# Experts' limits by bisection: marks on GpSimd, counts in TensorE, one step a group, and the weights' scaling on ScalarE

## What is computed

```
xn  = layernorm(x)
out = x + attention(xn) + experts(xn)
# attention: 16 heads of 16, k, q, v = xn @ W_kqv + b; causal, with slopes[h] * (j - i)
# added to the scores; softmax; y @ W_proj + b_proj
# experts: probs = softmax(xn @ Wg) over 8 experts, T = 4096 tokens, cap = T // 8 = 512
_, top_idx = top_k(probs.T, cap)          # each expert marks its 512 likeliest tokens
tok2exp = likeliest expert among those that marked the token, else the likeliest of all
out += probs[t, tok2exp] * gelu(xn @ W1[e]) @ W2[e]      # F = 512, for e = tok2exp[t]
```

## Time and profile before

| what | us |
| --- | --- |
| median of 3 runs | 610.05 |
| lowest, highest | 603.38, 613.67 |
| the profiled execution | 612.12 |
| its span in the trace | 610.4 |

### The profile page before, as it was taken

The page is one execution under the profiler, slowest core; times in us unless marked ns, Lnnn a source line. Parts: engine busy times, 40 slices in busy tenths (PEclk is TensorE's granted clock), DMA queues, the critical chain, the costliest instruction groups (busy, mean ns, idle before and its releaser), DMA issues.

```text
span 610.4 us, 13176 instructions
## 1 busy us (share of the span) xinstructions
PE 500.1 (82%) x4807; PEld 287.9 (47%) x4807; DVE 406.3 (67%) x829; ACT 324.6 (53%) x608; POOL 400.1 (66%) x556
## 2 busy tenths in 40 slices
PE   1989996578878889889888987887897798787876
PEld 1555652223334435344344444443356587665764
DVE  5887669998998897988998967530113545344543
ACT  4455651055656665766756646555643445353542
POOL 4877627567666796876867878884413476555555
PEclk9999997568989999999999899898699999888999
DMA  8999988322424432524325236538445344443510
GB/s 262 270 240 280 318 280 277 107 62 62 124 63 120 137 122 88 159 79 134 97 81 150 80 118 204 185 93 304 126 88 130 89 102 107 96 94 94 101 53 34
DMA packets 94902, 85.58 MB, mean 140 GB/s; under 512 B 36883, under 2 KB 84883, under 8 KB 94831
## 3 DMA queue, kind: packets, MB, share of 16 engines
q1 hardware_dynamic: 82088, 59.64, 34.2%
q0 software_dynamic: 7360, 18.80, 10.5%
q10 hardware_dynamic: 5392, 6.31, 3.4%
HBM read 42.26 MB, written 37.95 MB: 131 GB/s over the span
## 4 chain that ended last, share of the span: by engine, by line
PE 45%; DVE 34%; issue 10%; ACT 5%; POOL 3%; another core or an unknown queue 2%; DMA 1%; DVEq 0%; ACTq 0%; POOLq 0%
DVE mx L987 14%; PE ps L1378 8%; PE ps L1246 8%; PE ps L1358 5%; PE ps L1408 5%; PE ps L1540 4%; DVE mx L982 4%; PE ps L1530 3%; PE ps L1531 3%; PE ps L1283 2%; DVE pr_all L1204 2%; DVE pr_all L1209 2%; ACT pr_all L857 2%; PE ps L1353 2%
## 5 line engine op out<-in xcount | busy, mean ns | idle before, releaser
L857 ACT ACTIVATE pr_all<-ps 128x512 f32<-128x512 f32 x320 | 179.2, 597 | 124.9 <-PE ps L1358 110.1
L987 DVE TENSOR_REDUCE mx<-ps 128x2 f32<-128x768 f32 (+1 forms) x192 | 156.3, 862 | 15.6 <-PE ps L1283 7.9
L1358 PE MATMUL ps<-qs,ks 64*128 64x384 f16 (+3 forms) x512 | 110.6, 318 | 10.2 <-ACT pr_all L857 9.3
L711 POOL TENSOR_SCALAR_AFFINE_SELECT pr_all<-pr_all 128x256 f32<-128x256 f32 (+1 forms) x168 | 70.1, 445 | 67.0 <-ACT pr_all L857 66.4
L1378 PE MATMUL ps<-pr_all,vt 128*17 128x512 f32 (+3 forms) x1024 | 88.1, 462 | 3.2 <-issue 1.6
L1277 PE MATMUL ps<-step,pick 64*128 64x128 bf16 (+1 forms) x640 | 55.8, 220 | 29.8 <-DVE mx L987 21.9
L1540 PE MATMUL ps<-vt,pr_all 128*128 x312 | 62.7, 288 | 21.2 <-DVE pr_all L1209 20.2
L1283 PE MATMUL ps<-ks,qs 64*128 64x128 f16 (+3 forms) x512 | 77.1, 327 | 0.0
L1204 DVE TENSOR_TENSOR pr_all<-ps,pr_all 128x512 f32<-128x512 f32 x39 | 27.0, 691 | 72.3 <-ACT pr_all L879 39.7
L750 POOL DMA_INDIRECT out_dram<-pr_all,token x39 | 43.2, 1107 | 45.4 <-DVE pr_all L1215 32.0
L1530 PE MATMUL ps<-pr_all,xnp 128*128 128x256 f16 x312 | 61.1, 286 | 3.4 <-DVE pr_all L1204 2.7
(11 more groups left out here) (195 smaller groups left out, 945.0 us busy)
## 6 DMA issues: line engine op xcount, KB each, us to landing
qs<-q_parts SPq DMA_DIRECT2D x64, 100.0 KB
ks<-k_parts SPq DMA_DIRECT2D x64, 96.0 KB
sorted_rows<-ecmp POOLq DMA_DIRECT2D x10, 516.0 KB, 6.4
k_parts<-pr_all SPq DMA_DIRECT2D x16, 256.0 KB, 2.8
q_parts<-pr_all SPq DMA_DIRECT2D x16, 256.0 KB, 2.8
w_h<-in_L_ffn_W_dram SPq DMA_DIRECT2D x16, 256.0 KB
w_l<-in_L_ffn_W_dram SPq DMA_DIRECT2D x16, 256.0 KB
expert_parts<-w_low SPq DMA_DIRECT2D x32, 128.0 KB
```

The costliest lines, as they stand in the source:

```text
L711: pool.affine_select(out=v, in_=v, compare_op=ALU.is_ge, fill=0.0, base=0, pattern=[[0, blocks], [1, P]], channel_multiplier=-1).then_inc( ...
L857: act.activation(dst, src, ACT.Exp, scale=SCORE).then_inc(exp_made, 1)
L987: last = dve.tensor_reduce(mx[:, n1 % 2, :, 2 * g + c, t], ps[:, 2 * (u % 2):2 * (u % 2) + 2, c0:c0 + w], AX, ALU.max)
L1358: last = pe.matmul(dst[:, c0:c0 + w], ks[rows, p, 2 * g + i, t * P:(t + 1) * P], qs[rows, p, 2 * g + i, t * P:S], start=not masked, stop=T ...
```

## The change

The search's steps move to one a group: step `it` begins in slot 1 of group `it`, so there are four each in batches 0 to 2 and three in batch 3. VectorE now makes only the three candidates and signals `cand_made`. GpSimd, at the start of the group's work, waits for them and writes three sets of marks (128x256 in bfloat16 each) with one comparison each. TensorE counts: eight matmuls of three times 32 columns, accumulated in 96 columns of bank 7, in slot 6 (slot 9 where g = 3). VectorE's take, a slot later, first adds the 96 columns up to three numbers and then goes on as before. `expert_high` goes to ScalarE, in two instructions: the high part behind the exponential k = 1, the scaling in place behind k = 5; the four early quarters stand on ScalarE ahead of the first exponential, the last two of them behind the DMA issue of the shift's half. Three waits for bank 7 come or move. The assignments and declarations that are left out only name the new tiles and the new semaphore.

```
-STEPS = [(0, u) for u in (1, 8, 15, 22, 29, 36)] + [(n, u) for n in range(1, ROUTED) for u in (2, 8, 14)]
+STEPS = [(it // NG, NSJ * (it % NG) + 1) for it in range(BITS // 2)]
-TOTAL_AT = {at_slot(n, u + 5): it for it, (n, u) in enumerate(STEPS)}
-TAKE_AT = {at_slot(n, u + 6): it for it, (n, u) in enumerate(STEPS)}
+TOTAL_AT = {at_slot(n, u + (8 if it % NG == NG - 1 else 5)): it for it, (n, u) in enumerate(STEPS)}
+TAKE_AT = {at_slot(n, u + (9 if it % NG == NG - 1 else 6)): it for it, (n, u) in enumerate(STEPS)}
...
-            def expert_high(q):
-                j = q % 2
-                pool.wait_ge(we_in[j], 16 * (q // 2 + 1))
-                after(pool, we_out[j], 32 * min(q // 2, X) + 16 * max(q // 2 - X, 0))
-                pool.tensor_scalar(high_part(q), wq[j], WS, None, ALU.mult)
-                pool.tensor_scalar(wq[j], wq[j], WS, None, ALU.mult).then_inc(we_hi, 1)
...
             for q in range(NQ):
-                expert_high(q)
                 expert_low(q)
...
+                    if G < BITS // 2:
+                        pool.wait_ge(cand_made, G + 1)
+                        after(pool, tot_made, G)
+                        for j in range(3):
+                            last = pool.tensor_scalar(marks3[:, j, :], prt, cand[:, j:j + 1], None, ALU.is_ge)
+                        last.then_inc(cnt_made, 1)
                     for i in range(2):
...
-                        if i == 0 and n < X - 1:
-                            expert_high(NQ * (n + 1) + g)
...
+            def expert_high(q):
+                act.wait_ge(we_in[q % 2], 16 * (q // 2 + 1))
+                after(act, we_out[q % 2], 32 * min(q // 2, X) + 16 * max(q // 2 - X, 0))
+                act.activation(high_part(q), wq[q % 2], ACT.Copy, scale=WS)
+
+            def expert_scale(q):
+                act.activation(wq[q % 2], wq[q % 2], ACT.Copy, scale=WS).then_inc(we_hi, 1)
...
-            act.wait_ge(c_made, 1)
-            shift_half(act, 0, 1)
+            for q in range(NQ):
+                if q == 2:
+                    act.wait_ge(c_made, 1)
+                    shift_half(act, 0, 1)
+                expert_high(q)
+                expert_scale(q)
...
+                        if k == 1 and n < X - 1:
+                            expert_high(NQ * (n + 1) + g)
+                        if k == 5 and n < X - 1:
+                            expert_scale(NQ * (n + 1) + g)
...
             def bisect_count(it):
-                mark(dve.tensor_tensor(cand[:, :].bitcast(U32), thr[:, :].bitcast(U32).broadcast_to([P, 3]), bits[:, it, :],
-                                       ALU.bitwise_or))
-                with nc.allow_low_precision("counts up to 256 are exact"):
-                    for j, marks in enumerate((hit, gtb, third)):
-                        last = dve.tensor_scalar(marks[:, :, :], prt_e, cand[:, j:j + 1], None,
-                                                 ALU.is_ge, ALU.add, accum_out=cnt1[:, j:j + 1])
-                last.then_inc(cnt_made, 1)
+                dve.tensor_tensor(cand[:, :].bitcast(U32), thr[:, :].bitcast(U32).broadcast_to([P, 3]), bits[:, it, :],
+                                  ALU.bitwise_or).then_inc(cand_made, 1)
...
                 dve.wait_ge(tot_made, it + 1)
-                mark(dve.tensor_scalar(acc[:, :], bank[7][:, 384:387], float(CAP), None, ALU.is_ge, ALU.add, accum_out=met[:, :]))
+                mark(dve.tensor_reduce(sum3[:, :], bank[7][:, 384:480].rearrange("p (j n) -> p j n", j=3), AX, ALU.add))
                 dve.sem_inc(tot_read, 1)
+                mark(dve.tensor_scalar(acc[:, :], sum3[:, :], float(CAP), None, ALU.is_ge, ALU.add, accum_out=met[:, :]))
...
                 pe.wait_ge(cnt_made, it + 1)
-                pe.matmul(bank[7][:, 384:387], own[:, :], cnt1[:, :], start=True, stop=True).then_inc(tot_made, 1)
+                for c in range(8):
+                    last = pe.matmul(bank[7][:, 384:480], own[:, :], marks3[:, :, 32 * c:32 * c + 32], start=(c == 0), stop=(c == 7))
+                last.then_inc(tot_made, 1)
...
                             after(pe, xadd_made, TB * n - 2)
+                            if n == 0:
+                                pe.wait_ge(tot_read, 3)
                             turn_max(n + 1)
...
                             pe.wait_ge(c_made, n + 1 + g // 3)
+                            if g == NG - 1:
+                                after(pe, xadd_made, TB * n)
                             total(TOTAL_AT[n, g, k])
...
-                                pe.wait_ge(tot_read, len([a for a in STEPS if a < (n, 2 * NSJ)]))
+                                pe.wait_ge(tot_read, NG * n + 3)
```

More of the change, by code:

```diff
@@ L203, in layer @@
         cand = sb("cand", [P, 3], F32)
-        cnt1 = sb("cnt1", [P, 3], BF16)
+        marks3 = sb("marks3", [P, 3, X * NT], BF16)
+        sum3 = sb("sum3", [P, 3], F32)
         hit = sb("hit", [P, X, NT], BF16)
@@ L298, in layer @@
         pj_made, xadd_made = sem("pj_made"), sem("xadd_made")
-        cnt_made, tot_made = sem("cnt_made"), sem("tot_made")
+        cand_made, cnt_made, tot_made = sem("cand_made"), sem("cnt_made"), sem("tot_made")
         rt_dve, rt_pe = sem("rt_dve"), sem("rt_pe")
```

## The result

The changed kernel takes 633.67 us (median of 4 runs, 630.90 to 638.82) where the kernel before takes 609.66 (603.38 to 613.67): a ratio of 1.0432, with an interval of 1.0378 to 1.0486. It is 4.3% slower. The forecast was 604 us with a range of 591 to 616; time and sign are both outside it. The profiled execution took 634.6 us, its span is 632.9.

A forecast was written before the change was run, and what follows sets the result against it. No engine bound throughout: VectorE in batch 0 and first halves of batches, TensorE in second halves. Terms -5.5 - 4.2 - 1 + 2 + 3.5 - 1 = -6.2 us, carried to the median of 610.05, gave 604 us; range 591 to 616.

The forecast's parts named there:

- the wait at the total: TensorE waiting for GpSimd's three marks before counting: 0.3 to 0.5 us in a normal group, counted as nothing.
- the margin above: Slack in first halves of batches 1 to 3, like today's 20 us against VectorE's 19.06, meant to cover normal waits.
- the three steps behind the bias: Groups whose marks follow GpSimd's bias addition: marks some 2 us late, three times, put at +2 us in all.
- B: Rival: marks late in every group, total waiting 2.5 us in each of 15 groups; +18 us, 628; chance 0.08.
- the 14.3 taken from VectorE: VectorE's saving in the search from dropping the marking passes: 0.95 us a step over 15 steps, at most 14.3 us.
- Batch 0: -5.5: First attention batch: four search steps instead of six, VectorE loses 8.6 us, TensorE then binds; -5.5 us.
- Batches 1 to 3: -1.4 each: Attention batches: first half -1.8 us by VectorE's relief, second half +0.4; -1.4 a batch, -4.2 for three.
- ScalarE: +3.5: Weight conversions among the exponentials: 0.25 us of each of 28 behind k=1 shows, half hidden; +3.5 us (0 to 15.7).
- Rival C: ScalarE sets the pace: every conversion behind k=1 costs its full 0.56 us, +15.7; 616 us; chance 0.09.
- The stretched operations: -1: Two tiny two-input VectorE operations a step, stretched most likely by GpSimd: 0 to 2.5 us back, taken as 1.
- VectorE's net relief of a step: Search step on VectorE: three marking passes of 1.29 us go, reduction and wait of 0.36 come; 0.95 us taken.
- The sum without the waits: Forecast terms for batches, stretched operations, ScalarE and GpSimd's lag (-1), without the +2 us for late marks.

The follow-up runs named there:

- e8: Kernel after with one GpSimd marking pass instead of three (limits found differ) and the bias added behind the next group's marks: 602.22 us, ratio 0.9858.
- e4: Kernel after with the bias of batches 0, 2 and 3 added behind the next group's marks instead of ahead: 626.28 us, ratio 1.0247.
- e1: Kernel before with only the weights' conversions moved from GpSimd to ScalarE, search untouched: 609.38 us, ratio 1.0033.
- e10: Kernel before with the tiny candidates and limits operations written as one tensor and a per-partition scalar: 601.98 us, ratio 0.9885.
- e5: Kernel after with totals in slots 8, 8, 6, 9 instead of 6, 6, 6, 9, takes one slot behind: 621.38 us, ratio 1.0163.
- e13: e11 with candidates made in slot 0, right behind the take (first step stays in slot 1), totals kept: 600.90 us, ratio 0.9890.
- e6: Kernel after with the edits of e4 and e5 together: 623.11 us, ratio 1.0200.
- e11: e6 with the candidates and limits operations written as one tensor and a per-partition scalar: 605.65 us, ratio 0.9971.
- e14: Kernel after with only candidates and limits written as one tensor and a per-partition scalar, on another chip: 576.66 us, ratio 1.0342.

## Why the prediction was wrong

**The step that failed** is the wait at the total. The prediction compared 209.7 us, when the marks would be ready, with 209.40, when TensorE gets to the total, and wrote "a wait of 0.3 to 0.5 us in a normal group", "within the margin above". Two numbers in it were off.
- The marks. From the start of the candidates to the first matmul of a total that waits, the kernel after takes 3.12 us: 0.25 until GpSimd starts, 2.73 for the three marks, 0.14 to hand over (213.94, 214.19, 216.92, 217.06). The prediction had 2.4, three marks of 0.8 and no hand-over. A mark took 921 ns; half the columns of the earlier trace rows cost 0.62 of the time.
- TensorE's arrival. One reading of the trace of before, 2.1 us behind the candidates, stood for all steps. In the kernel after TensorE is there 1.6 us behind them in group 0 of batches 1 to 3 (idle from 215.55, where the candidates start at 213.94), 2.0 to 2.4 us behind them in the other steps that wait, and 6 us or more behind them where the total stands in slot 9. e8, in which nothing waits, has 1.5, 1.9 to 2.3 and 6 or more. So in group 0 the reading was 0.5 us too late; that VectorE's relief brought TensorE forward there is likely, but no run shows it apart.

Together that is 0.8 to 1.5 us in an ordinary step and 2.7 to 3.1 behind the bias, and not 0.4 and 2; in groups 1 and 2 the marks' time alone makes the wait. And the waits of the ordinary steps, 10.1 us in nine, stood in the sum as nothing. By the ratios, of the 4.3 points e4 gives 1.9 to the three steps behind the bias, where the prediction's term was +2 us in all, and 2.4 to the rest, where it had none.

**The rival that came true was B**, the marks that are late in every group: its time, 628, was the nearest, and it had 0.08. Its mechanism was right, with TensorE's total waiting and the maxima and ScalarE starving behind it. Its point of deciding, 3.3 us for three marks, was too high: it decided at 2.73, and the price that it named was for marks of 1.49 us, which didn't come. So that 628 is near is in part luck. The waits sum to 18.6 us where it had 37; but they aren't made up for by the 14.3 taken from VectorE, and TensorE goes on at the lower clock after some of them, which stood in no term. How much of the 24 us is the clock wasn't separated from the waits by any run, and stays open; the trace only shows both in one place.

**Batch 0: -5.5.** e8 has it without waits: -8.8 against the trace of before, -5.4 against that of e1. The term was about right; in the kernel after the waits ate it.

**Batches 1 to 3: -1.4 each.** Wrong. e8, where nothing waits for marks, gains nothing there. VectorE's relief (2.3 us a batch) and TensorE's extra 1.4 us meet in slots in which neither is full. Batch 4, which has no step of the search, takes 39.9 us before and 39.5 after as well. What sets the 40 us, this study doesn't show.

**ScalarE: +3.5, within 0 to 15.7.** e1 gives +0.3%, that is 2 us with an interval of -1 to 5, though a conversion takes 0.62 us and not 0.56. Rival C is out.

**The stretched operations: -1.** The mechanism was named ("most likely GpSimd"), with 2.5 us at most. e10 measures what it is worth in the kernel before: 1.15% or 7 us, with an interval of 1 to 13, so probably more than the 2.5 us by which the medians exceed the shortest. Why more, no run shows; at the low end of the interval it isn't more. In the kernel after the line's median fell from 311 to 195 ns by itself, and its longest, 711 ns, stayed.

**The prices of the other single operations** nearly held. The reduction was put at 0.25 us; the eight matmuls at 0.32 to 0.45, and they take 0.50 at full clock. VectorE's net relief of a step has a slip in its arithmetic: 1.29 - 0.36 - 0.03 is 0.90, and the 0.93 to 0.96 that stands there adds the 0.03; over 15 steps that is less than 1 us. The durations' view of the kernel after:

```profile
L711 POOL TENSOR_SCALAR marks<-rr,cand x45: 911/921/932, 123.6 to 288.3; 128x256 bf16<-128x256 f32 x45
...
L1079 DVE TENSOR_REDUCE sum<-ps x15: 245/247/248, 129.3 to 291.6; 128x3 f32<-128x96 f32 x15
```

**The sum without the waits** was -5.5 - 4.2 - 1 + 3.5 - 1 = -8.2 us; e8 has 602.22 - 608.58 = -6.4 by the medians and -8.6 by the ratio. The size is right, but partly by luck: batches 1 to 3 gave nothing of their -4.2, and ScalarE cost less than its +3.5. What turned a gain of 6 us into a loss of 24 was one thing, the waits at the totals, put at +2 us for three steps and at nothing for the others, and worth 30 by the medians.

## What to carry to other kernels

When work moves to a slower engine off the path, its result has a time at which another engine asks for it. Take that time for each place in which it asks (here 1.6, 2.0 to 2.4 or over 6 us behind the candidates), allow for the asking engine to come sooner once others are relieved, and set the whole chain against it, hand-overs included (here 3.12 us). Price a wait of the engine that feeds all others with what stands in its queue behind it, and ask later for the result or start its making earlier (e5, e13) before moving it. And look at tiny two-input operations on VectorE beside a busy GpSimd: rewriting two of them gave 1.15% (0.2 to 2.1), as much as any version of this change that counts all three candidates.

## What the runs showed of the hardware

- A VectorE operation with two tensors in SBUF can stand until GpSimd's running row ends: 159 ns undisturbed, up to 1.04 us in e6 for a single column. With one tensor and a per-partition scalar it takes 212 to 216 ns every time (e10, e11, e13). That is no full cure: in e13 the same form with three columns took between 219 and 944 ns. The Trainium skill (GPSIMD Engine Reference, § 1 Specifications) names two SBUF inputs as a case of contention; the trace agrees, and shows that it is a hold of up to 0.9 us. One such row in e13 ends with GpSimd's as well (219.74 and 219.71 us):

```profile
218.56 1.15 POOL L677 TENSOR_TENSOR w_low<-w_l 128x512 f16<-128x512 f32 x1
...
218.80 0.94 DVE L1076 TENSOR_SCALAR cand<-bits,thr 128x3 uint32<-128x3 uint32 x1
```

- A GpSimd comparison of 256 columns takes 921 ns, the scaling of 512 took 1488: by these two, which differ in operation and output type as well, an estimate of 350 ns that doesn't depend on the columns. On VectorE the same marks take 354 ns, and with the accumulator 0.40 or more on the chain.
- TensorE's clock can fall behind waits of 0.8 as well as of 2.7 us, and then the matmuls that should catch up run at the lower level for some microseconds (0.72 and 0.61 in the windows above). The length of the wait alone doesn't decide it: in the kernel after the eight matmuls of a total take 0.80 us behind a wait of 0.79 (180.50) and 0.50 us behind one of 1.51 (217.06).
- The chip of the fourth group runs the kernel before in 8% less time (557.67 us against 603.5 to 609.7). e14's span there is 56.3 us shorter than that of the kernel after; 37 us of it are the stage behind the last copy of attention (155 us in the kernel after, 118 in e14), 17 are batches 5 to 7, and only 2.4 lie ahead of the end of batch 3. The waits of the kernel after in the experts' stage, 478 to 633 us:

```profile
DVE pr_all L1213 <- ACT pr_all L892: 46.8, 27, 5.4
...
ACT pr_all L892 <- remote: 29.6, 12, 5.1
DVE pr_all L1213 <- issue: 24.7, 10, 4.3
```

and those of e14, 458 to 577 us:

```profile
DVE pr_all L1214 <- ACT pr_all L892: 33.1, 35, 1.1
```

On the chip of the kernel after single waits last up to 5.4 us, and some have no releaser in the profile; on the other the same wait is never above 1.1. Why, nothing here shows. It doesn't touch the comparison, which has both kernels on one chip, and the ratio of e14 there is near that of the kernel after.
